# The second layer's sums: windows that begin at a group's lowest receiver, carries as a matrix product, and a table in node order that is loaded plainly

## What is computed

```
h      = x @ W                                  # 3125 x 256, four heads side by side
e      = leaky_relu(attn_src[src] + attn_dst[dst]) * edge_weight
e_exp  = exp(e - max(e))
denom  = segment_sum(e_exp, dst)
alpha  = e_exp / (denom[dst] + 1e-10)
out    = segment_sum(h[src] * alpha, dst)       # 3125 x 256
x      = layernorm(x + out)
```

## Time and profile before

| | us |
|---|---|
| median of 3 runs | 2392.39 (2390.41 to 2396.98) |
| the profiled execution | 2400.63 |
| its span | 2398.6 |
| mean granted TensorE clock in it | 0.892 |

### The profile page before, as it was taken

The page is one execution under the profiler, slowest core; times in us unless marked ns, Lnnn a source line. Parts: engine busy times, 40 slices in busy tenths (PEclk is TensorE's granted clock), DMA queues, the critical chain, the costliest instruction groups (busy, mean ns, idle before and its releaser), DMA issues. The chain is left out here.

```text
span 2398.6 us, 38205 instructions
## 1 busy us (share of the span) xinstructions
PE 1909.3 (80%) x12132; PEld 1633.2 (68%) x12132; DVE 1425.6 (59%) x4037; ACT 1208.7 (50%) x2298; POOL 1519.2 (63%) x1253
## 2 busy tenths in 40 slices
PE   7799999989999999999999999966145555555560
PEld 6688888878888888888888888855033444444440
DVE  6556666556666666666666666646164554554575
ACT  2477677666777777777777777744000000000012
POOL 0417677777777777777777777752745655655623
PEclk9899999999999999999999999988567777667785
DMA  7788877777777777777777877766434544444433
GB/s 245 254 224 185 176 164 165 142 150 171 163 159 161 160 160 161 166 158 159 159 161 167 176 171 173 162 107 194 113 94 118 128 118 128 128 117 129 127 82 110
DMA packets 239708, 370.94 MB, mean 155 GB/s; under 512 B 33256, under 2 KB 172482, under 8 KB 239496
## 3 DMA queue, kind: packets, MB, share of 16 engines
q0 software_dynamic: 104688, 191.38, 40.0%
q1 hardware_dynamic: 134807, 177.00, 25.9%
HBM read 260.28 MB, written 107.97 MB: 154 GB/s over the span
## 5 line engine op out<-in xcount | busy, mean ns | idle before, releaser
L1548 POOL DMA_INDIRECT accA<-ystage,to_a x391 | 642.4, 1643 | 217.0 <-issue 113.3
L1554 POOL DMA_INDIRECT GA<-TA,src_c x391 | 429.7, 1099 | 252.3 <-issue 111.8
L1605 POOL DMA_INDIRECT Hg<-HT,src_c x391 | 375.0, 959 | 255.7 <-DVE xb L1117 147.5
L643 DVE TENSOR_TENSOR h2l<-h2f,h2h 128x512 fp32r<-128x512 f32 (+1 forms) x294 | 203.0, 690 | 314.1 <-ACT h2h L1998 160.1
L1680 PE MATMUL bank<-h1h,W1h 128*128 128x512 f32 x882 | 354.7, 402 | 11.0 <-DVE h1l L643 11.0
L2035 ACT ACTIVATE h1f<-bank 128x512 f32<-128x512 f32 (+1 forms) x392 | 221.0, 590 | 256.9 <-PE bank L1735 196.8
L1682 PE MATMUL bank<-h1h,W1l 128*128 128x512 f32 x882 | 349.1, 396 | 0.0
L1681 PE MATMUL bank<-h1l,W1h 128*128 128x512 f32 x882 | 349.0, 396 | 0.0
L2178 ACT ACTIVATE drop<-neg_m 128x1 f32<-128x1 f32 x49 | 14.4, 295 | 603.6 <-issue 418.3
L1927 PE MATMUL bank<-xb,in_window 128*128 128x260 f32 (+1 forms) x782 | 279.7, 518 | 47.6 <-issue 47.2
L643 DVE TENSOR_TENSOR h1l<-h1f,h1h 128x512 fp32r<-128x512 f32 x294 | 194.3, 688 | 117.8 <-ACT h1h L1998 107.5
(11 more groups left out here) (252 smaller groups left out, 4490.6 us busy)
## 6 DMA issues: line engine op xcount, KB each, us to landing
ef<-in_eT SPq DMA_DIRECT2D x97, 256.0 KB
bcast_i<-in_src_row SPq DMA_DIRECT2D x97, 256.0 KB
TW<-TB SPq DMA_DIRECT2D x116, 203.0 KB
HB<-hist SPq DMA_DIRECT2D x98, 130.0 KB
rel<-RL SPq DMA_DIRECT2D x97, 128.0 KB
rem<-RD SPq DMA_DIRECT2D x48, 256.0 KB
TB<-stB SPq DMA_DIRECT2D x24, 406.0 KB
accA<-zeros SPq DMA_DIRECT2D x4, 2193.0 KB, 16.4
```

Of the source, the lines that this page charges most:

```text
L643: return dve.tensor_tensor(o, full, hi.bitcast(f32), ALU.subtract)
L1548: return pool.indirect_dma_start(out=table, out_offset=bass.IndirectOffsetOnAxis(ap=rows, axis=0), in_=sums, in_offset=None, compute_op=AL ...
L1554: pool.indirect_dma_start(out=GA[0:n, b % (GAR * BLOCKS_PER_GROUP), :].bitcast(f32), out_offset=None, in_=TA, in_offset=bass.IndirectOffse ...
L1605: pool.indirect_dma_start(out=Hg[0:n, slot, :], out_offset=None, in_=HT, in_offset=bass.IndirectOffsetOnAxis(ap=src_c[0:n, b:b + 1], axis= ...
```

## The change

- A window's row is the receiver minus the group's lowest receiver (`rel_c`), not the number modulo 128.
- The sums of a window go to a table F in DRAM in node order: group g's 128 rows are stored at the row of its lowest receiver, an address that SP loads into a register. Stores overlap, so each waits until the one before it has landed (`s_hd`).
- A window's carry is a fifth product in PE's accumulation: `to_next`, a unit matrix shifted by the distance between the two lowest receivers (for even g times `drop`), times the `hist` of the window before. DVE makes `to_next` (128x128) from a constant in PSUM; `carry_window`'s reading of PSUM, `drop_k` and `keep` go.
- ACT copies the sums from PSUM to `hist` (`window_copy`), with the window's running maximum as a 261st column, and signals `s_carry`.
- `last_rows`, `factor`, `chosen`, `scale` go.
- At the end SP loads the 261st column of all nodes in one DMA (`row_m`, 3200 elements of 4 B), then `fin` in six plain DMAs; POOL's 25 gathers go. ACT makes `row_eps` from the column, and the division uses max(row_eps, 1e-10).
- `attention_residual` multiplies and adds in one operation for each tile and head (100 of 128x64), in place of products into PSUM and additions. `attention_factors` has two small operations a chunk.

```diff
-            const(dve.tensor_single_scalar(rem_ci[:, :], dst_c[:, :], P - 1, ALU.bitwise_and))
-            const(dve.tensor_copy(rem_c[:, :], rem_ci[:, :]))
...
+            const(dve.tensor_scalar(moved[:, 1:NG], steps[:, 1, 1:NG], p_f[:, :], None, ALU.add))
+            const(dve.tensor_tensor(rel_c[:, 0:FULL]..., dst_f[:, 0:FULL]..., low[...]..., ALU.subtract))
...
-            def carry_window(g):
-                q = g // 2
-                if g % 2 == 0:
-                    dve.wait_ge(s_drop, q + 1)
-                    dve.tensor_tensor(drop_k[:, q:q + 1], drop[:, q:q + 1], keep[:, g:g + 1], ALU.mult).then_inc(s_dk, 1)
-                dve.wait_ge(s_S, g + 1)
...
-                dve.scalar_tensor_tensor(hist[:, g % HISTR, 0:BW], hist[:, (g - 1) % HISTR, 0:BW], carried,
-                                         PS[g % 3][:, 0:BW], ALU.mult, ALU.add).then_inc(s_carry, 1)
-            def last_rows():
...
+            def carry_matrix(g):
+                if g == 0:
+                    return
+                if g >= 3:
+                    dve.wait_ge(s_S, g - 1)
+                o, shifted = to_next[:, g % 2, :], moved[:, g:g + 1]
+                if g % 2:
+                    dve.tensor_scalar(o, iota_p, shifted, None, ALU.is_equal).then_inc(s_next, 1)
+                    return
+                dve.wait_ge(s_drop, g // 2 + 1)
+                dve.tensor_scalar(o, iota_p, shifted, drop[:, g // 2:g // 2 + 1], ALU.is_equal, ALU.mult).then_inc(s_next, 1)
...
                 if 0 <= q < NQ:
                     weighted_rows(2 * q)
-                if 0 <= q - 1:
-                    carry_window(2 * q - 2)
+                    carry_matrix(2 * q)
...
                     weighted_rows(2 * q + 1)
-                if 0 <= q - 1:
-                    carry_window(2 * q - 1)
+                    carry_matrix(2 * q + 1)
...
-                if q == ADC // 4:
-                    last_rows()
...
+                for t in tiles:
+                    n = rows_of_tile(t)
+                    for h in range(HEADS):
+                        w = slice(h * HD, (h + 1) * HD)
+                        last = dve.scalar_tensor_tensor(xn[0:n, t, w], fin[0:n, t, w], cinv[0:n, t, h:h + 1], xn[0:n, t, w],
+                                                        ALU.mult, ALU.add)
+                    last.then_inc(s_res, 1)
...
                     for g in (2 * q, 2 * q + 1):
+                        first = sp.value_load(low_i[0:1, g:g + 1], min_val=0, max_val=N - 1)
                         sp.wait_ge(s_carry, g + 1)
-                        sp.dma_start(HB[g * P:(g + 1) * P, :], hist[:, g % HISTR, :]).then_inc(s_hd[g % HISTR], 16)
+                        if g == 0:
+                            sp.wait_ge(s_zrow, 32)
+                        else:
+                            sp.wait_ge(s_hd, 16 * g)
+                        sp.dma_start(F[bass.ds(first, P), :], hist[:, g % HISTR, :]).then_inc(s_hd, 16)
...
+            wait_windows_stored(sp)
+            sp.dma_start(row_m[:, :], F[0:NT * P, BW:FW].rearrange("(t p) d -> p (t d)", p=P),
+                         allow_slow_non_contiguous=True).then_inc(s_rowm, 16)
+            for c in range(NC):
+                tiles = tiles_of_chunk(c)
+                sp.dma_start(fin[:, tiles[0]:tiles[-1] + 1, :],
+                             F[tiles[0] * P:(tiles[-1] + 1) * P, 0:BW].rearrange("(t p) d -> p t d", p=P)).then_inc(s_fin[c], 16)
...
                     last = pe.matmul(PS[g % 3][:, 0:BW], in_window[0:n, j, :], xb[0:n, j, :],
-                                     start=b == blocks[0], stop=b == blocks[-1])
+                                     start=b == blocks[0], stop=g == 0 and b == blocks[-1])
+                if g >= 1:
+                    pe.wait_ge(s_next, g)
+                    pe.wait_ge(s_carry, g)
+                    last = pe.matmul(PS[g % 3][:, 0:BW], to_next[:, g % 2, :], hist[:, (g - 1) % HISTR, 0:BW],
+                                     start=False, stop=True)
                 last.then_inc(s_S, 1)
...
+            def window_copy(g):
+                act.wait_ge(s_S, g + 1)
+                if g >= HISTR:
+                    act.wait_ge(s_hd, 16 * (g - HISTR + 1))
+                copy(hist[:, g % HISTR, 0:BW], PS[g % 3][:, 0:BW])
+                copy(hist[:, g % HISTR, BW:FW], neg_m[:, g // 2 + 1:g // 2 + 2]).then_inc(s_carry, 1)
...
             for q in range(NQ):
+                if q >= 2:
+                    window_copy(2 * q - 4)
+                    window_copy(2 * q - 3)
                 act.wait_ge(s_nm, q + 1)
...
+            act.wait_ge(s_rowm, 16)
+            act.activation(row_eps[:, :], row_m[:, :], ACT.Exp, bias=log_eps[:, :]).then_inc(s_factor, 1)
```

More of the change, by code:

```diff
@@ L322, in build_program @@
         drop = sb("drop", [P, NQ], f32, sc)
[L323 to L327, removed]
+        row_m = sb("row_m", [P, NT], f32, sc)
+        row_eps = sb("row_eps", [P, NT], f32, sc)
+        log_eps = sb("log_eps", [P, 1], f32, sc)
         Wc = sb("Wc", [P, DK, OUT + 2 * HEADS], f32, sc)
@@ L499, in build_program @@
         s_S = sem("s_S")
-        s_dk = sem("s_dk")
+        s_next = sem("s_next")
         s_carry = sem("s_carry")
-        s_hd = [sem(f"s_hd{i}") for i in range(HISTR)]
+        s_hd = sem("s_hd")
+        s_rowm = sem("s_rowm")
         s_nd = sem("s_nd")
@@ L615, in wait_windows_stored @@
         def wait_windows_stored(eng):
[L616 to L617 removed]
+            eng.wait_ge(s_hd, 16 * NG)
         def if_outside(eng):
@@ L1252, in _ @@
                 dve.wait_ge(s_vht, 16 * NT + 32)
-                step(dve.memset(scale[:, :], 1.0))
-                step(dve.tensor_scalar(row_i[:, :], n_f[:, :], float(ACC0), None, ALU.add), "rows")
-                step(dve.tensor_scalar(trash_u[:, :], trash[:, :], float(ACC0), None, ALU.add))
+                step(dve.memset(neg_m[:, NQ:NQ + 1], 0.0))
+                step(dve.memset(hist[:, 0, BW:FW], 0.0), "rows")
                 for b in range(NB):
@@ L1311, in attention_residual @@
-                for j in range(0, k, 2):
-                    m = min(2, k - j)
-                    last = weigh(bank[3 * (c % 2) + j // 2][:, 0:m * OUT].rearrange("p (t d) -> p t d", d=OUT),
-                                 fin[:, t0 + j:t0 + j + m, 0:OUT], factors[:, j:j + m], P, m)
-                last.then_inc(s_att, 1)
+                dve.wait_ge(s_cinv, NC + c + 1)
+                for t in tiles:
[5 more added lines that the diff above has]
+                    last.then_inc(s_res, 1)
@@ L1666, in _ @@
                         pool.wait_ge(s_vs, 16 * (NB + b))
-                    add_to_table(HB, to_u[0:n, :], hist[0:n, 0, :]).then_inc(s_vs, 16)
+                    add_to_table(F, to_u[0:n, :], hist[0:n, 0, :]).then_inc(s_vs, 16)
                 pool.wait_ge(s_vs, 32 * NB)
-            for t in range(NT):
-                pool.indirect_dma_start(
-                    out=fin[:, t, :], out_offset=None, in_=HB,
-                    in_offset=bass.IndirectOffsetOnAxis(ap=row_i[:, t:t + 1], axis=0)).then_inc(s_fin[[t in tiles for tiles in CHUNKS].index(True)], 16)
         @block.tensor
@@ L2189, in _ @@
                 last.then_inc(s_ex, 1)
-            for i in range(2):
-                last = act.activation(factor[:, :].rearrange("p (q i) -> p q i", i=2)[:, :, i], neg_m[:, 1:NQ + 1], ACT.Exp,
-                                      bias=neg_m[:, NQ:NQ + 1], scale=-1.0)
-            last.then_inc(s_factor, 1)
+            for g in range(NG - 4, NG):
+                window_copy(g)
             with if_outside(act):
```

115 lines of the change are left out of this document (40 added, 75 removed).

## The result

The changed kernel takes 2398.24 us, the median of 20 runs, against 2390.51 us for 20 runs of the kernel before: a ratio of 1.0031 (95% interval 1.002 to 1.0042), some 7.4 us slower by the ratio and 7.7 by the medians. The profiled execution took 2397.13 us, its span is 2395.3 and its mean granted clock 0.898.

The account below looks back on a forecast made before the run. DVE and POOL take turns: gather burst, score operations, weighing, next burst. Terms -6.6 (`last_rows`), -1.2 (pairs that pick scores) and -1.1 (whole end) sum to -8.9, rounded to -8.4: 2392.4 to 2384.0 us, range 2370 to 2404.

Parts of the forecast that it names:

- The carry in a regular pair: 0: Edge loop: the fifth product (0.50 to 0.95 us) is covered by 4.9 us before DVE uses the scores' products; 0 us.
- Rival D: Edge loop: PE's scores end DVE's idle time, so the product adds 0.50 to 0.95 us a pair; 2406 or 2426; 0.13.
- The median execution hasn't most of the stall: End: the profile's 10.1 us stall is mostly absent from the median, 8.2 us below the profile, so removing it gains nothing.
- Rival B: End: the stall belongs to POOL's 25 gathers and goes with them, saving 10.1 us more; 2373.9 us; chance 0.22.
- `last_rows`: Around the fourth pair in the edge loop: removing this list from DVE saves 6.6 us, bounds 4 and 8.87.
- Pairs that pick scores: Edge loop, six passes where DVE has no idle time to speak of: 0.2 us saved in each, -1.2 us.
- The end's first part: From the last carry to DVE's start at the end: store, SP's branch, column and first `fin` load; +0.6 us.
- rival C: End: the column of 3200 elements moves slowly, 17.9 us instead of 4; 2396.4 us; chance 0.14.
- The end's second part: DVE's chunks at the end: 6.6 us per five tiles, 38.6 us from DVE's start to the end; headed -1.2 us.

Follow-up runs that it names:

- experiment 2: Kernel after without the carry (no fifth product on PE, no `carry_matrix` calls on DVE; copies and serial stores stay): 2376.06 us, ratio 0.9929.
- 3: Kernel before with a fifth product of zeros added to every window, no new wait: 2425.01 us, ratio 1.0125.
- experiment 5: Kernel before with the product of zeros in even windows only, queued behind the products for the scores: 2383.9 us, ratio 1.0005.
- 6: Kernel before with the product of zeros in odd windows only, queued ahead of the products for the scores: 2415.87 us, ratio 1.0127.
- experiment 12: Kernel after with 25 gathers that nothing needs put back on POOL at the end: 2408.44 us, ratio 1.006.
- experiment 1: Kernel after with PE's products for the scores of pair q+3 queued ahead of the sums of window 2q+1: 2376.89 us, ratio 0.9936.
- experiment 7: Kernel after with the products for the scores queued between the four blocks of window 2q+1 and its carry product: 2364.34 us, ratio 0.9917.
- experiment 11: Kernel after with DVE's `weighted_rows(2q+1)` and its `carry_matrix` ahead of `edge_scores(q+2)`, and PE's `spread_maxima` behind window 2q+1's sums: 2403.77 us, ratio 1.0089.
- experiment 9: Kernel before with the fourth gather of every group left out from group 12 on, six gathers a pair instead of eight: 2312.36 us, ratio 0.97.

## Why the prediction was wrong

Forecast were 2384.0 us, 8.4 faster, with 0.54 for faster; the kernel is 7.4 slower, inside the range and on the other side. Point by point:

- **"The carry in a regular pair: 0" is the step that failed.** The product has about the size that was taken for it (1.06 and 0.60 us by the records, 0.95 and 0.50 taken), and its cover was put at 4.9 us, from the records of L1907 to the moment DVE goes on. That wasn't slack. While a burst of gathers is under way DVE goes on late, at a moment that depends on when PE came to these products. Measured: +5.6 us for seven pairs, 0.80 a pair, of which 4.5 go with the carry (experiment 2); two more passes ahead of the signal do the same to the kernel before, and cost nothing behind it (3, 5 and 6). The loop is 21.2 us longer although `last_rows`, 6.3 us, is out of it: 27.5 us for this step, of which 24 go with the carry by the ratio of experiment 2. Rival D had the place and the price (0.50 to 0.95 us a pair) but the wrong threshold: I let it decide only once L1907 ended later than the burst, and gave it 0.13.
- **"The median execution hasn't most of the stall" failed too**, with the opposite sign. The 8.2 us between profile and median are within the scatter of the point at which the second layer starts (1650.7 to 1671.0 us, part of it between chips). The stall is in the profiles of the kernel before and of all its variants with the fifth product (22.7 to 22.9 us for the two chunks, 62.6 to 64.7 from the last store's issue to the end), and 12 shows its cause. Rival B was right: 10.1 us gained.
- `last_rows`: -6.6 forecast, -6.3 measured.
- Pairs that pick scores: -1.2 forecast. These pairs and the one behind them take 27.14 us (7.12 + 20.02) instead of 26.95 (7.18 + 19.77), so +0.2 each: a miss without weight.
- The end's first part: +0.6 forecast, -5.1 measured. The store's landing and SP's way past its branch took 4.0 us together where I added 4.46 and 4.3; from the column's issue to the first rows of `fin` it was 5.2 where I took 6.2. The term that was mis-sized is SP's start: in the kernel before POOL's wait for the stores stands ahead of its branch, in the new one SP's stands behind it, and SP comes to the branch (L611) at 2348.53, right behind its last store, and passes it while that store is under way.
- The column of 3200 elements of 4 B had landed 3.5 us after its issue, and rival C's 17.9 of transfer is far off. The rule of the Trainium skill, "DMA: Bandwidth & Descriptors", "Rules for kernel authors", by which each element becomes a descriptor and the transfer is to be rearranged, has no price, and here there was nothing to gain by following it.
- The end's second part: chunks of 6.6 forecast, 6.65 measured, and 37.9 us from DVE's start to the end where 38.6 was forecast. The heading's -1.2 is a slip: 38.6 against 2388.5 - 2348.21 = 40.3 is -1.7, and with the +0.6 that gives the -1.1 of the sum. Twenty operations of 128x64 take 4.00 us, 0.20 each, where I had 0.196 from the rows of 128x256. The estimate of 0.127 from the Trainium skill, "VectorE: DVE Perf Modes", "The TRN2 errata — SBUF-src ops pay a fixed extra latency per instruction", was too low.
- Sum as measured: +21.2 in the loop and -17.5 at the end, +3.7, or +23.6 and -16.0, +7.6, against the profile of experiment 5; the medians have +7.7.

B and D together, worked out as they stood, give 2406 - 10 = 2396, near the 2398. They weren't exclusive, and I had priced them one at a time.

## What to carry to other kernels

The time from an instruction's record to the moment its waiter goes on isn't slack unless a row shows what the waiter waits for; here "remote" stood in that place, and the work put in front of it, a product of 0.60 to 1.06 us, cost 0.8 us a pair. Where one engine's queue holds both a product on which the whole loop turns and one that nobody awaits soon, queue the former first: the same carry product behind the scores' products instead of ahead of them turned a loss of 7 us into a gain of 20. A stall that lies beside gathers and ends soon after them may be theirs (here it went with them), and belongs in the sum of a change that takes them away.

## What the runs showed of the hardware

While POOL's indirect gathers follow each other back to back, operations of other engines start late: DVE behind PE (the scores at 2280.34, 6.5 us after the products' records had ended), ACT behind PE (2280.35), DVE behind itself (experiment 12) and PE between the products of one window (experiment 1). Not in the first microseconds of a burst: the copy at 2273.30, 4.5 us into one, started at once. And not always until it ends: in two bursts with 1.3 us between them in experiment 7 (2063.93 to 2085.3) the products for the scores had ended by their records at 2068.53 and the scores started at 2072.68, with POOL still issuing. It can outlast the burst: by 2.8 us in experiment 12, by 3.1 in experiment 11. In experiment 12 the late operations start in steps of 0.70 us or twice that, and the regular pairs' periods lie about as far apart, 12.6 to 12.8, 13.3 to 13.5 and 14.0 to 14.2 us. Without gathers beside it the same list of DVE operations has no such gap.

That the gathers are behind it is shown by taking some away (experiment 9) and by adding some (12). What in them does it is open. In every run the issuing on POOL and the moving of the gathered rows come together, so neither is shown to be the cause; and the records can't tell an instruction whose signal comes late from one that its engine starts late. Why it takes some microseconds to show, no run here tells.
